# Causal attention with its tail in pieces and seven tiles' routing in it, and a dense feed-forward with shifted units

## What is computed

```python
# layer 1, feed-forward (weights are dequantized and merged beforehand)
y2 = relu(x1 @ w_up + b_up) @ w_down + b_down
# layer 2, feed-forward
h = rmsnorm(x, ln1_w)
q, k, v = ((h @ w).reshape(b, s, 16, 128) for w in (wq, wk, wv))
attn = softmax(where(causal, q @ k.T / sqrt(128), -1e9))
x = x + (attn @ v).reshape(b, s, 2048) @ wo
t = rmsnorm(x, ln2_w).reshape(-1, d)
probs = softmax(t @ gate_w.T)                      # 16 experts
topv, topi = top_k(probs, 6); topv = topv / sum(topv)
cw = zeros((T, 16)).at[rows, topi].add(topv)       # routing weights ("shares")
routed = sum over e of (silu(t @ eg_w[e]) * (t @ eu_w[e]) * cw[:, e]) @ ed_w[e]
out = x + routed + (silu(t @ sg_w.T) * (t @ su_w.T)) @ sd_w.T
```

## Time and profile before

| what | value |
|---|---|
| runs | 4305.97, 4312.45, 4316.2 us, median 4312.45 |
| profiled run | 4308.22 us |
| its span | 4306.5 us |
| granted TensorE clock over the span | 0.948 |
| TensorE busy | 3818.6 us (89%) |
| VectorE, ScalarE, POOL busy | 2617.0, 1997.2, 901.2 us |
| `ffn4` | about 1373 to 1675.5 us |
| `mha` | 1675.5 to 2732.5 us |
| `moe2a` | 2732.5 to 3219.5 us |

### The profile page before, as it was taken

How to read it: one execution, slowest core, us unless ns; L and a number is a source line. 1 busy time by engine, 2 the same in 40 slices (tenths; PEclk the granted TensorE clock), 3 DMA queues, 4 the chain that set the end, 5 groups by cost and what they waited for, 6 DMA issues and landing times. The chain is left out here.

```text
span 4306.5 us, 76239 instructions
## 1 busy us (share of the span) xinstructions
PE 3818.6 (89%) x26248; PEld 3246.2 (75%) x26248; DVE 2617.0 (61%) x5941; ACT 1997.2 (46%) x5211; POOL 901.2 (21%) x743
## 2 busy tenths in 40 slices
PE   6776999999998886999999999699989998898791
PEld 5655888888776775788888888588878887676670
DVE  7878999999577554555555555444434333777533
ACT  6885666666322443444433443333333332886140
POOL 1113333333101441000000000122322333111245
PEclk9997999999999997999999999899999999998695
DMA  2001000000002111111111111322223221003144
GB/s 72 18 13 47 1 0 0 0 0 1 25 22 76 44 56 64 52 38 40 41 38 36 38 40 40 100 75 70 72 66 105 75 74 59 16 15 93 58 135 129
DMA packets 149757, 209.49 MB, mean 49 GB/s; under 512 B 20800, under 2 KB 87648, under 8 KB 149216
## 3 DMA queue, kind: packets, MB, share of 16 engines
q1 hardware_dynamic: 142608, 187.14, 14.1%
q0 software_dynamic: 6864, 18.75, 1.6%
HBM read 178.18 MB, written 27.66 MB: 48 GB/s over the span
## 5 line engine op out<-in xcount | busy, mean ns | idle before, releaser
L1572 ACT ACTIVATE peer_tab<-peer_sims 128x128 f32<-128x128 f32 x1024 | 305.6, 393 | 0.0
L1579 POOL TENSOR_TENSOR peer_tab<-peer_sims 128x2048 f32<-128x2048 f32 x64 | 247.0, 3880 | 276.9 <-ACT peer_sims L1556 248.5
L1627 DVE SCALAR_TENSOR_TENSOR peer_tab<-peer_tab,peer_th 128x2048 f32<-128x2048 f32 x128 | 298.3, 2373 | 2.6 <-ACT peer_tab L1572 2.3
L1644 PE MATMUL bank<-ident,peer_tab 128*128 128x128 f32 x2048 | 247.9, 275 | 23.7 <-DVE peer_tab L1627 23.7
L1644 PEld LDWEIGHTS bank<-ident,peer_tab 128*128 128x128 f32 x2048 | 234.5, 142 | 37.1 <-DVE peer_tab L1627 24.6
L1694 PE MATMUL bank<-peer_wd,peer_hh 128*128 128x256 f32 x1024 | 246.3, 384 | 2.4 <-DVE peer_hh L1685 2.4
L1667 PE MATMUL bank<-peer_hT,peer_wg 128*128 128x256 f32 x1024 | 244.3, 382 | 0.0
L952 DVE TENSOR_TENSOR moe2a_b<-moe2a_a,moe2a_spread 128x512 f32<-128x512 f32 x104 | 78.6, 756 | 235.7 <-ACT moe2a_a L926 232.6
L1667 PEld LDWEIGHTS bank<-peer_hT,peer_wg 128*128 128x128 f32 x1024 | 195.8, 191 | 27.1
L952 DVE TENSOR_TENSOR moe2b_b<-moe2b_a,moe2b_spread 128x512 f32<-128x512 f32 x96 | 68.0, 708 | 234.6 <-ACT moe2b_a L926 232.9
L1694 PEld LDWEIGHTS bank<-peer_wd,peer_hh 128*128 128x128 f32 x1024 | 184.8, 190 | 30.9 <-DVE peer_hh L1685 7.4
(11 more groups left out here) (502 smaller groups left out, 10942.8 us busy)
## 6 DMA issues: line engine op xcount, KB each, us to landing
mha_wo<-mha_wo SPq DMA_DIRECT2D x128, 256.0 KB, 2.6
moe2b_spread<-moe_shares SPq DMA_DIRECT2D x48, 256.0 KB, 3.1
moe2a_spread<-moe_shares SPq DMA_DIRECT2D x40, 256.0 KB, 3.3
m_y_rows<-moe_y SPq DMA_DIRECT2D x79, 128.0 KB, 1.7
att_ctxT<-in_ctxT_dram SPq DMA_DIRECT2D x32, 256.0 KB, 2.6
lin_ctxT<-in_ctxT_dram SPq DMA_DIRECT2D x16, 256.0 KB, 2.6
ffn_in_gq<-in_ctxT_dram SPq DMA_DIRECT2D x16, 256.0 KB, 2.6
ffn_in_gq<-in_ctx_dram SPq DMA_DIRECT2D x16, 256.0 KB, 3.0
```

What stands on the lines that cost most here:

```text
L1572: i = nc.scalar.activation(tab[g][h][:, b * P:(b + 1) * P], sims[:, g, 1, h, :], ACT.Identity, bias=sims[:, g, 0, h, b:b + 1])
L1579: nc.gpsimd.tensor_tensor(out=tab[g][h][:].rearrange("p (a b) -> p a b", b=P), in0=sims[:, g, 1, h, :].unsqueeze(1).broadcast_to([P, NB, P ...
L1627: nc.vector.scalar_tensor_tensor(out=tab[g][h][:], in0=tab[g][h][:], scalar=th[:, g, h:h + 1], in1=tab[g][h][:], op0=ALU.is_ge, op1=ALU.mu ...
L1644: i = nc.tensor.matmul(TB[n % 2][:, j * P:(j + 1) * P], tab[g][h][:, blk * P:(blk + 1) * P], core.ident[:], start=(j == 0 and h == 0), sto ...
```

## The change

In `mha` the tail is in pieces. VectorE's five are after heads 2, 3, 4, 5 and 6, TensorE's and ScalarE's halves of the transposes after heads 7 and 8. The front's pieces move by one head (7, 8, 9) and its halves stand after heads 10 and 11. The routing weights of the tile before are new in this stage, for tiles 0 to 6: logits after head 9, exp after 10, the rest of VectorE's chain after 12, transposes and copy after 13, store after 14, in bank V too. `moe2a` makes only the last tile's weights, during tile 6, and its tile 0 makes none. The gate weights are loaded ahead, in ffn4. At the start of `mha`, POOL, ScalarE, VectorE and TensorE take their steps in another order, and at its end too. Projections take hT_hi with both weight parts before hT_lo. In `ffn4` the late unit's transposes move from slot 1 to 2, its readout and residual from 2 to 3, the front's halves stand in slots 3 and 4, and the low part in 6. (The table of slots and the helpers' new arguments are cut here to what differs.)

```diff
     def slot_pe(pe, t, j):
         n, late = 2 * (t - 1), 2 * (t - 1) - 1
-        if j == 1 and exists(late):
+        if j == 2 and exists(late):
             transpose_pe(pe, late)
-        if j == 2 and exists(late):
+        if j == 3 and exists(late):
             readout_pe(pe, late)
...
@@ -443,7 +443,7 @@
             stats_dve(dve, n)
         if j == 2 and exists(n):
             rows_dve(dve, n)
-        if j == 2 and exists(late):
+        if j == 3 and exists(late):
             residual_dve(dve, late)
         if j == 3 and exists(n):
...
 
-    NORM, TRANS, LOGITS, ROUTER, WEIGHTS, LOW = 0, 3, 4, 5, 8, 9 if gated else 4
...
+        if ln and not peer and TRANS <= j < TRANS + C:
+            transposes_pe(pe, t, (j - TRANS,))
+        if routed(t) and j == LOGITS:
             logits_pe(pe, t)
-        if routed and j == WEIGHTS and not is_first(t):
+        if routed(t) and j == WEIGHTS:
             cwT_pe(pe, t)
         if peer and j in SCORES:
...
                 loaded_act(act, 0, 0)
-                split_act(act, 0, GATE_UP)
-                if routed:
-                    router_act(act, 0)
-                    cwT_act(act, 0, 0)
-                split_act(act, 0, DOWN)
+                split_act(act, 0)
             else:
...
 
 
-    TAIL_DVE, TAIL, FRONT_STATS, FRONT_MS, FRONT_ROWS, FRONT = 3, 5, 6, 7, 8, 9
+    TAIL_ROWS, TAIL_ADD, TAIL_STATS, TAIL_MS, TAIL_SCALE, TAIL = 2, 3, 4, 5, 6, 7
...
     def project_pe(pe, t, s):
         total = t * NH + s
         if s == 0:
-            pe.wait_ge(hT_ready, t + 1)
+            pe.wait_ge(hi_handed, t + 1)
         if isinstance(t, int) and t == 0 and s % QUAD == 0:
-            pe.wait_ge(lo_made, (s // QUAD + 1) * NS)
+            pe.wait_ge(lo_made, s // QUAD * NS + RAWS)
         for w, out, ready, copied in ((wqs, Q, q_ready, qs_ready), (wks, K, k_ready, ks_ready)):
             if some(total):
                 pe.wait_ge(copied, total)
-            for n, (pw, ph) in enumerate(((0, 0), (0, 1), (1, 0))):
+            for n, (pw, ph) in enumerate(((0, 0), (1, 0), (0, 1))):
+                if s == 0 and w is wqs and ph == 1:
+                    pe.wait_ge(hT_ready, t + 1)
                 for c in range(C):
                     i = nc.tensor.matmul(out[:], w[pw][:, c, s * HD:(s + 1) * HD], hTs[ph][:, c, :],
                                          start=(n == 0 and c == 0), stop=(n == 2 and c == C - 1))
@@ -2042,10 +2040,16 @@
 
         if some(total):
             pe.wait_ge(v_emptied, total)
-        if s == TAIL + 1 and not (isinstance(t, int) and t == 0):
-            pe.wait_ge(t_emptied, t * C)
-        if s == FRONT + 1 and not (isinstance(t, int) and t == NT - 1):
-            pe.wait_ge(f_emptied, (t + 2) * C)
+        if isinstance(t, int) and t == 0 and s % QUAD == 0:
+            pe.wait_ge(lo_made, (s // QUAD + 1) * NS)
+        if s - TAIL in (1, 2) and not (isinstance(t, int) and t == 0):
+            pe.wait_ge(t_emptied, (t - 1) * C + s - TAIL)
+        if s == LOGITS + 1 and not (isinstance(t, int) and t == 0):
+            pe.wait_ge(l_emptied, t)
+        if s - FRONT in (1, 2) and not (isinstance(t, int) and t == NT - 1):
+            pe.wait_ge(f_emptied, (t + 1) * C + s - FRONT)
+        if s == SHARES + 1 and not (isinstance(t, int) and t == 0):
+            pe.wait_ge(w_emptied, t)
...
+    def tail_rows_dve(dve, t):
         tail_chain.begin(t)
-        dve.wait_ge(out_done, (t + 1) * NH)
         dve.wait_ge(mvb_ready, t + 1)
         dve.wait_ge(f_filled, (t + 2) * C if not (isinstance(t, int) and t == NT - 1) else NT * C)
         for g in range(GT):
             i = nc.vector.tensor_scalar(x1[:, g, :], group_x(t, g), mvb[:, g, 0:1], rstdb[:, g:g + 1], ALU.subtract, ALU.mult)
         i.then_inc(tail_chain.sem, 1)
+
+    def tail_add_dve(dve, t):
+        tail_chain.begin(t)
         dve.wait_ge(tail_chain.sem, tail_chain.next())
+        dve.wait_ge(out_done, (t + 1) * NH)
         for n in range(2):
             half = x1[:, 2 * n:2 * n + 2, :].rearrange("p g d -> p (g d)")
             i = nc.vector.tensor_tensor(out=half, in0=Y[n][:], in1=half, op=ALU.add)
         i.then_inc(tail_chain.sem, 1)
         dve.wait_ge(tail_chain.sem, tail_chain.next())
         dve.sem_inc(y_used, 1)
+
+    def tail_stats_dve(dve, t):
+        tail_chain.begin(t, 2)
         xt = x[:, bass.ds(t * (GT * D), GT * D)]
         nc.vector.tensor_tensor(out=xt, in0=xt, in1=x1[:].rearrange("p g d -> p (g d)"), op=ALU.add)
         for g in range(GT):
             i = nc.vector.bn_stats(stats2[:, g, :], x1[:, g, :])
         i.then_inc(tail_chain.sem, 1)
...
+    def tail_scale_dve(dve, t):
         dve.wait_ge(r2_ready, t + 1)
         for g in range(GT):
             i = nc.vector.tensor_scalar(x1[:, g, :], x1[:, g, :], r2[:, g:g + 1], None, ALU.mult)
         i.then_inc(tn_ready, 1)
-        tail_chain.end()
         if not (isinstance(t, int) and t == NT - 1):
             keep_stats_dve(dve, t + 1)
...
+    def logits_pe(pe, t):
+        pe.wait_ge(t_emptied, (t + 1) * C)
+        pe.wait_ge(v_emptied, (t + 1) * NH + LOGITS + 1)
+        for g in range(GT):
+            for c in range(C):
+                i = nc.tensor.matmul(V[:, g * E:(g + 1) * E], tT[:, c, g * P:(g + 1) * P], gw[:, c, :], start=(c == 0), stop=(c == C - 1))
+        i.then_inc(l_filled, 1)
+
+    def logits_dve(dve, t):
+        route_chain.begin(t)
+        logits = V[:, 0:GT * E].rearrange("p (g e) -> p g e", e=E)
+        dve.wait_ge(l_filled, t + 1)
+        nc.vector.tensor_reduce(out=rmax[:], in_=logits, axis=AX.X, op=ALU.max).then_inc(route_chain.sem, 1)
+        dve.wait_ge(route_chain.sem, route_chain.next())
+        nc.vector.tensor_tensor(out=shifted_l[:], in0=logits, in1=rmax[:].unsqueeze(2).broadcast_to([P, GT, E]),
...
+    def logits_act(act, t):
...
+    def route_dve(dve, t):
+        route_chain.begin(t, 1)
+        wide = [P, GT, E]
+        dve.wait_ge(l_exp, t + 1)
...
+        nc.vector.reciprocal(rmax[:], rsum[:]).then_inc(route_chain.sem, 1)
+        dve.wait_ge(route_chain.sem, route_chain.next())
+        dve.wait_ge(cw_init, 1)
+        if some(t):
+            dve.wait_ge(w_filled, t)
+        nc.vector.tensor_tensor(out=cw[:, :, 0:E], in0=picked[:], in1=rmax[:].unsqueeze(2).broadcast_to(wide), op=ALU.mult).then_inc(cw_done, 1)
+        route_chain.end()
+
+    def shares_pe(pe, t):
+        pe.wait_ge(cw_done, t + 1)
+        pe.wait_ge(v_emptied, (t + 1) * NH + SHARES + 1)
+        for g in range(GT):
+            i = nc.tensor.transpose(V[0:32, g * P:(g + 1) * P], cw[:, g, :], core.ident[:])
+        i.then_inc(w_filled, 1)
+
+    def shares_act(act, t):
+        act.wait_ge(w_filled, t + 1)
+        if some(t):
+            act.wait_ge(shares_stored, 16 * t)
+        nc.scalar.activation(cwT[:], V[0:32, :], ACT.Copy).then_inc(w_emptied, 1)
+
+    def shares_sp(sp, t):
+        sp.wait_ge(w_emptied, t + 1)
+        sp.dma_start(shares[0:32, bass.ds(t * TILE, TILE)], cwT[:]).then_inc(shares_stored, 16)
 
...
+
+    TAILS_DVE = {TAIL_ROWS: tail_rows_dve, TAIL_ADD: tail_add_dve, TAIL_STATS: tail_stats_dve, TAIL_MS: tail_ms_dve, TAIL_SCALE: tail_scale_dve,
...
         def _(pe):
-            front_pe(pe, 0)
-            tiles(pe, step_pe, {FRONT: front_pe}, tail_pe)
+            for c in range(C):
+                front_pe(pe, 0, c)
+            pe.wait_ge(inputs.norms_in, n_norms)
+            tiles(pe, step_pe, halves(FRONT, front_pe), {**halves(TAIL, tail_pe), LOGITS: logits_pe, SHARES: shares_pe})
             scores_pe(pe, NT - 1, NH - 1)
-            for l in (2, 1):
-                transpose_pe(pe, NT - 1, NH - l)
-            for l in (3, 2, 1):
+            transpose_pe(pe, NT - 1, NH - 2)
+            for l in (3, 2):
                 apply_pe(pe, NT - 1, NH - l)
                 out_pe(pe, NT - 1, NH - l - 1)
-            out_pe(pe, NT - 1, NH - 1)
-            tail_pe(pe, NT - 1)
+            transpose_pe(pe, NT - 1, NH - 1)
+            apply_pe(pe, NT - 1, NH - 1)
+            for l in (2, 1):
+                out_pe(pe, NT - 1, NH - l)
+            for c in range(C):
+                tail_pe(pe, NT - 1, c)
 
         @block.scalar
         def _(act):
-            split_act(act, 0)
+            split_act(act, 0, slice(0, RAWS))
             act.wait_ge(inputs.norms_in, n_norms)
+            for c in range(C):
+                front_act(act, 0, c)
+            split_act(act, 0, slice(RAWS, None))
             act.wait_ge(zeroed, 1)
-            front_act(act, 0)
-            tiles(act, step_act, {FRONT: front_act}, tail_act)
+            tiles(act, step_act, halves(FRONT, front_act), {**halves(TAIL, tail_act), ROUTE_EXP: logits_act, SHARES: shares_act})
             transposed_act(act, NT - 1, NH - 2)
             exp_act(act, NT - 1, NH - 1)
-            applied_act(act, NT - 1, NH - 3)
+            for l in (3, 2):
+                applied_act(act, NT - 1, NH - l)
             transposed_act(act, NT - 1, NH - 1)
```

(25 more changed lines are left out.)

208 lines of the change are left out of this document (116 added, 92 removed).

## The result

The changed kernel takes 4253.3 us (median of 4 runs, 4252.22 to 4256.03), beside 4310.24 us for the kernel before in the same comparison; the ratio is 0.9871, 95% interval 0.986 to 0.9883. A second comparison on another occasion, with 4 runs of it (median 4260.5) and 7 of before (4309.06), gave 0.9886 (0.987 to 0.9903). The prediction was 4253 us in a range of 4235 to 4279, and faster.

A forecast was written before the change was run, and what follows sets the result against it. TensorE was taken to bound attention and moe2a. Terms -18.8, -6.5, -3.4, -21.0 and -9.6 sum to -59.3 us: span 4306.5 becomes 4247.2, plus 1.7 and 4.2 gives 4253 us, range 4235 to 4279.

The forecast's parts named there:

- Attention tiles: Attention stage, all tiles: tail and front in halves save more than the added routing costs, -18.8 us.
- The attention's start: Start of the attention stage: first Q projection 8.1 us sooner, partly given back by heads 0 and 1, -6.5 us.
- Clears and memset: Attention's start: POOL's semaphore clears and memset come off the path ahead of tile 0's pow, 5.3 us.
- End of the attention and start of moe2a: Attention's end, row passes and last output blocks reordered, -3.4 us; moe2a's start and tile 0 without routing, -5.4 us.
- moe2a's tiles: moe2a tiles 1 to 5: they lose all routing, 3.12 us a tile, -15.6 us.
- Feed-forward: Dense feed-forward: split front's transposes, moved late unit and a last tile without its wait, -9.6 us, bounds -5 and -20.
- the 2.47 us: Feed-forward loop tiles: removing TensorE's wait for the unit's `pbd` gains nothing, as hh_lo's wait stands behind; bounds 0 and -2.5 a tile.
- the second: Start, drain and feed-forward give nothing, because weights, DMA and hh_lo's chain end where they did: 4272 us; chance 0.12.
- the first: Attention tiles: the pieces do not hide, V's bank makes projections wait, 5 x 0.6 us a tile: 4272 us; chance 0.15.
- the third: More is won: the feed-forward's 2.47 us wait shrinks by half in six tiles and clock dips go: 4241 us; chance 0.12.
- the fourth: Attention: routing weights not ready for their transposes after head 13, 10.4 us in each of seven tiles: 4326 us; chance 0.03.
- the table loads: moe2a: twelve fewer ScalarE table switches, 2.66 us each, all on the path, save 32 us: 4221 us; chance 0.02.

The follow-up runs named there:

- the lump: The changed kernel with VectorE's five tail pieces in one piece after head 3, TensorE's halves unmoved; ratio to the kernel before 0.9925.
- the later chain: The changed kernel with the rest of VectorE's routing chain after head 13 in place of 12; ratio to the kernel before 0.9965.
- The kernel without routing: The kernel before with the changed attention stage but no routing in it, moe2a and feed-forward as before; ratio to the kernel before 0.9902.
- the splits stood later: The changed kernel with attention tile 0's weight splits at the step's end on ScalarE and VectorE; ratio to the kernel before 0.9847.
- the slots-only kernel: The kernel before with only the feed-forward late unit's transposes in slot 2, readout and residual in 3; ratio to the kernel before 0.9997.
- second trace: The changed kernel run again, unedited; ratio to the kernel before 0.9886, span 4258.2 us.
- feed-forward kernels: The kernel before with the change's whole dense feed-forward part (late unit's slots, front's halves, low part) and nothing else; ratio to the kernel before 0.9979.

## Why the prediction was right

**The bound** (TensorE's own work and its stops, the other engines with room) was read rightly: of 54.0 us, 30 are standing time in the attention stage and 7 in moe2a, and where VectorE's work was placed badly (the lump, the later chain) TensorE's row moved by as much as the waits, or more.

**Attention tiles, -18.8 forecast, -16.1 measured.** Head 5's 4.0 us, head 9's 2.0, halves at 0.36 to 0.46 and logits at 1.8 came as summed; the predicted 124.55 is 124.2 to 124.7 in four tiles, 125.8 in one with a slow start, and 122.6 in tile 6, which ends without a jump. The kernel without routing measures the parts: 122.4, and about 2 for the routing. The pieces of the tail cost nothing, as booked. In tile 0 the -1.1 did not come: heads 8 and 9 still took 13.50 and 10.28 us, and 7.39 each once the splits stood later.

**The attention's start, -6.5 forecast, -2.6 measured.** This step failed. I let the first Q projection come 8.1 us sooner, and that was near (7.3), but gave only 1.6 of it back, with the V weights as the reason. What gave back was head 1's wait for ScalarE's copy of Q, 4.49 us where before there was none: the copy stands behind six splits whose raw loads have to land, and with the first Q 7.3 us sooner TensorE reaches it sooner. The row that would have told it is in the same list that I read, `mha_qs` 6.8 us in two waits (heads 5 and 9 of tile 0), which I left out of the sum. Clears and memset were priced at 5.3 as if all lay on the path; the clears cost 2.0.

**End of the attention and start of moe2a, -8.8 forecast, -11.1 measured**, the two terms together. TensorE at the seam, before and after:

```profile
2707.02 0.44 PE L2130 MATMUL bank<-ident,mha_pr 128*128 128x128 f32 x2 [3.14 <-DVEq L2120]
...
2725.95 1.11 PE L2248 MATMUL bank<-ident,mha_xr 128*128 128x128 f32 x4 [8.87 <-DVE mha_xr L2231]
...
2742.27 1.22 PE L859 MATMUL bank<-moe2a_hT_hi,moe2a_wg_hi 128*128 128x512 f32 x2 [1.69 <-DVE moe2a_wu_lo L1149]
...
2762.33 0.58 PE L877 MATMUL bank<-moe2a_wd_hi,moe2a_hh_hi 128*128 128x256 f32 x1 [11.67 <-POOL moe2a_hh_lo L940]
```

```profile
2698.46 1.12 PE L2262 MATMUL bank<-ident,mha_xr 128*128 128x128 f32 x4 [7.53 <-DVE mha_xr L2247]
2700.53 1.08 PE L2262 MATMUL bank<-ident,mha_xr 128*128 128x128 f32 x4 [0.95 <-ACT mha_hTf L2271]
2714.76 0.77 PE L858 MATMUL bank<-moe2a_hT_hi,moe2a_wg_hi 128*128 128x512 f32 x1 [13.15 <-DVE moe2a_wu_lo L1144]
...
2727.47 0.58 PE L876 MATMUL bank<-moe2a_wd_hi,moe2a_hh_hi 128*128 128x256 f32 x1 [4.57 <-POOL moe2a_hh_lo L937]
```

The end came as summed, -3.0 for -3.4. The 8.87 us wait became 7.53, which is the earlier trace rows's row passes of 1.38 out of the chain: "-1.4 surely" was that. The further 2.0 for the order of the last output blocks is 1.65: the last output block begins 18.43 us after the last head's Q, where it was 20.08, since the 3.14 us wait ahead of the last head's transposes is gone. What I sized too small is tile 0 of moe2a, 65.0 us in place of 73.2, whose second block takes 10.22 us in place of 17.31. TensorE's wait there is for hh_lo, 11.67 before and 4.57 after. VectorE's splits of the weights end 4.9 us sooner after the first G, since no router's chain stands among them any more. Behind them VectorE waited for the loads of `spread`, and that wait is gone:

```profile
2758.78 0.69 DVE L952 TENSOR_TENSOR moe2a_b<-moe2a_a,moe2a_spread 128x512 f32<-128x512 f32 x1 [3.09 <-DMA moe2a_spread<-moe_shares]
```

I had named this second part in the prediction and given it no number. Which share each of the two has was not measured by a run of its own. The wait that now opens moe2a, 13.15 us, ends with VectorE's low part of the U weights, but that stands behind hT_lo, and this behind the rows that come back from DRAM:

```profile
2709.72 1.06 ACT L652 ACTIVATE moe2a_hT_hi<-moe2a_hTf 128x1024 fp32r<-128x1024 f32 x1 [7.30 <-DMA moe2a_hTf<-t_scratch]
```

ScalarE then waits 0.77 us more for a piece of the weights, so rows and weights both bind this start.

**moe2a's tiles, -15.6 forecast and measured**, and tile 6 keeps its 57.5.

**Feed-forward, -9.6 forecast, -8.3 measured.** That the 2.47 us would be worth nothing because hh_lo stands behind POOL's pow is what the slots-only kernel showed (34.5 before and after, 2.33 for hh_lo). The split's -0.65 a tile was -1.2 and -1.1 in tiles 1 and 2 and -0.3 in tiles 3 to 6; the last tile gave 3.5 for 4.4. So most loop tiles are at 34.2 and not at the 33.8 of the forecast, and the clock tells why. Behind the same wait for hh_lo, 2.32 us in tile 2 (33.4 us) and 2.34 in tile 4 (34.2 us), the columns of the earlier trace rows are

```profile
1457.70:1459.40 1.70, 1.66 (x13) 1.66 (x14) 1.70 (x6) 0.00 (x0) 0.00 (x0) 1.00 0.04 10
1525.30:1527.00 1.70, 1.65 (x7) 1.65 (x8) 1.70 (x6) 0.00 (x0) 0.00 (x1) 0.50 0.00 0
```

Tiles 3 to 6 have the 0.50, and in the second trace all of tiles 2 to 6 have a clock below 1 there and take 34.2. In the slots-only kernel it is 1.00 in four of these five tiles. Why the fall comes more often here was not settled.

**The sum** was 5.3 us too large; 2.5 of it is the later start ahead of all that was changed. That the number fits to 0.3 us is luck. The forecast added 4.2 us to go from the profiled run to the median of the runs, as before's runs gave it; the changed kernel's median lies 1.0 below its profiled run (4253.3 and 4254.28). These 5.2 us cancel the 5.3. In the second comparison the median is 4260.5, 7.5 us above the forecast and within its range. Of the rivals, part of the second happened (the start gave 2.6 of 6.5); the first, the third and the fourth did not, and the table loads, given 0.02, are out.

## What to carry to other kernels

A wait taken away pays only if the next one on the same engine is not already standing behind it: before booking it, follow the next operations' producers one and two places back in the order of their own engine, as here hh_lo behind a pow of another chain. Work hung into a full pipeline was free here when it came in pieces smaller than a step's slack (VectorE's five, 7.39 us a head with and without them), and dear when it ended just ahead of its reader: one head's distance was worth 40 us. And where an early start is moved forward, look at the copies behind it in each engine's order: here a split that waited for its load held up the copy of Q behind it, for 4.49 us of TensorE's time. Last, when a forecast fits, check its terms one by one against the rows; here two errors of 5 us met.

## What was not expected of the hardware

After a loop's jump, TensorE's first head took 7.5 us in most tiles and 8.9 to 10.4 in none to two of a trace, in different ones each time. The clock behind the stop differs. Two starts, a slow one and another, in the second trace of the changed kernel, tiles 3 and 2:

```profile
2059.40:2062.40 3.00, 3.00 (x8) 2.39 (x9) 0.61 (x2) 0.40 (x1) 0.00 (x0) 0.58 0.12 41
1934.90:1937.90 3.00, 3.00 (x13) 2.51 (x14) 0.76 (x2) 0.60 (x1) 0.00 (x0) 1.00 0.18 61
```

The stop before the first was 1.79 us, before the second 1.60, and the granted clock was 0.58 behind the one and 1.00 behind the other. The lumped tail's 1.9 us waits cost 2.24 in six tiles and 3.77 in the last. Over the traces of all kernels the 18 slow starts stand behind stops of 1.78 to 2.92 us and the 52 others behind 1.43 to 2.52. So a stop of about 2 us may or may not cost 1.6 us more; why it falls on one tile and not on another was not settled.

An undisturbed head takes 7.41 us before, in the slots-only and feed-forward kernels and in the one without routing, and 7.39 in all kernels with routing in the attention, over 8 tiles some 2 us. The matmuls are the same; no run told what makes the 0.02.
